# A residual sum and a value scaling moved ahead of one part of a triangular inverse in VectorE's program, in steps 2, 6 and 10

## The reference

```python
x = x + _L0_attn_ref(_layernorm(x), Wq, Wk, Wv, Wb, conv_q, conv_k, conv_v, norm_w, Wo)
x = x + _L0_ffn_ref(_layernorm(x), gate_w, expert_up_w, expert_down_w, shared_up_w, shared_down_w)

# attention: 8 heads of 64
q, k, v = (silu(conv4(x @ W)) for W in (Wq, Wk, Wv)); q, k = l2norm(q), l2norm(k)
beta = sigmoid(x @ Wb)
for each token:                                   # delta rule, S is 64 x 64 for each head
    u = beta * (v - k S); S = S + k^T u; o = q S
o = o * rsqrt(mean(o * o) + 1e-5) * norm_w;  return o @ Wo

# experts: softmax gate, 2 of 4 groups, 4 of 16 experts for a token, and a shared expert
out = sum_e cw[:, e] * (swiglu(x @ up[e].T) @ down[e].T) + swiglu(x @ shared_up.T) @ shared_down.T
```

## Time and profile before

| | us |
|---|---|
| median of three runs | 1312.88 (1310.01 to 1314.16) |
| the profiled execution | 1310.06 |
| its span, first to last instruction | 1308.3 |
| TensorE busy (matmuls) | 1263.4 |
| VectorE busy | 866.1 |
| ScalarE, GpSimd busy | 372.0, 337.8 |
| mean granted TensorE clock, share of full | 0.989 |

### The profile page before, as it was taken

One profiled execution on the slowest core, in us unless ns is written; L12 is line 12 of the kernel. 1 busy time (PEld: TensorE's weight loads), 2 busy tenths in 40 slices (PEclk: granted clock), 3 DMA queues, 4 the chain that ended last, 5 costly groups with the idle time before them and its releaser, 6 DMA issues.

```text
span 1308.3 us, 27847 instructions
## 1 busy us (share of the span) xinstructions
PE 1263.4 (97%) x8725; PEld 786.9 (60%) x8726; DVE 866.1 (66%) x2411; ACT 372.0 (28%) x818; POOL 337.8 (26%) x398
## 2 busy tenths in 40 slices
PE   7979999999999999999999999999999999999997
PEld 6857778777876565444444555555555555555553
DVE  4897698769769328363111777777777777777774
ACT  4745555655553232120000111111111111111111
POOL 1302224313242222125651112122222222121212
PEclk9989999999997999999999999999999999999999
DMA  5534943843653794585457366666665656564420
GB/s 163 91 51 97 140 112 91 170 111 78 131 122 115 169 209 105 123 265 206 177 215 248 83 132 137 131 140 137 136 140 130 137 131 135 127 139 72 75 49 9
DMA packets 208517, 171.09 MB, mean 131 GB/s; under 512 B 71473, under 2 KB 160561, under 8 KB 208433
## 3 DMA queue, kind: packets, MB, share of 16 engines
q1 hardware_dynamic: 135056, 114.16, 34.2%
q0 software_dynamic: 16496, 34.23, 13.3%
q10 hardware_dynamic: 56880, 21.54, 7.9%
HBM read 91.06 MB, written 82.73 MB: 133 GB/s over the span
## 4 chain that ended last, share of the span: by engine, by line
PE 55%; DVE 2%; issue 0%; DMA 0%; POOL 0%; ACT 0%; DVEq 0%; POOLq 0%
PE pD L2311 15%; PE pG L2286 14%; PE pU L2295 14%; PE pG L2243 3%; PE pU L2243 3%; PE pD L2262 3%; PE pU L2237 1%; PE pD L2257 0%; DVE ups L2184 0%; DMA out<-y,ix 0%; DVE w L1884 0%; DVE w L1885 0%; DVE route_keep L1883 0%; POOL out L2076 0%; DVE qf L1896 0%
## 5 line engine op out<-in xcount | busy, mean ns | idle before, releaser
L2184 DVE STREAM_TRANSPOSE ups<-a 32x96 f32<-32x96 f32 (+1 forms) x1248 | 326.1, 261 | 42.4
L2076 POOL DMA_INDIRECT out<-y,ix x79 | 123.0, 1557 | 478.9 <-ACT y L2137 313.8
L2311 PE MATMUL pD<-w,ups 128*128 (+1 forms) x474 | 216.6, 593 | 0.7 <-DVE ups L2184 0.7
L2295 PE MATMUL pU<-w,xsT 128*128 x632 | 199.9, 459 | 0.0
L2286 PE MATMUL pG<-w,xsT 128*128 x632 | 199.9, 459 | 0.0
L2286 PEld LDWEIGHTS pG<-w,xsT 128*128 128x128 f32 x632 | 119.6, 189 | 88.2 <-issue 37.6
L2295 PEld LDWEIGHTS pU<-w,xsT 128*128 128x128 f32 x632 | 120.3, 190 | 66.7
L974 PE MATMUL pProj<-front_region 128*128 128x256 f32 x624 | 154.2, 390 | 2.2 <-ACT front_region L711 1.6
L2311 PEld LDWEIGHTS pD<-w,ups 128*128 128x128 f32 (+1 forms) x474 | 90.2, 191 | 93.0 <-issue 76.7
L974 PEld LDWEIGHTS pProj<-front_region 128*128 128x128 f32 x624 | 113.1, 191 | 19.9 <-ACT front_region L711 2.1
L2137 ACT ACTIVATE y<-pD,wq 128x512 f32<-128x512 f32 x79 | 54.3, 687 | 245.3 <-PE pD L2311 235.8
(11 more groups left out here) (258 smaller groups left out, 1650.6 us busy)
## 6 DMA issues: line engine op xcount, KB each, us to landing
w<-in_up_T SPq DMA_DIRECT2D x16, 1408.0 KB, 6.9
slot_rows<-zeros SPq DMA_DIRECT2D x79, 266.0 KB, 6.8
xs<-slot_rows ACTq DMA_DIRECT2D x316, 64.0 KB
w<-in_down_T SPq DMA_DIRECT2D x16, 512.0 KB, 8.8
front_region<-in_L_attn_hidden_states SPq DMA_DIRECT2D x16, 256.0 KB, 3.7
x2r<-in_L_attn_hidden_states SPq DMA_DIRECT2D x16, 256.0 KB, 4.4
partial_sums<-x2r SPq DMA_DIRECT2D x16, 256.0 KB, 3.0
x_normed<-x2n SPq DMA_DIRECT2D x16, 256.0 KB, 2.1
```

The costliest lines, as they stand in the source:

```text
L2076: pool.indirect_dma_start(out=flat, out_offset=bass.IndirectOffsetOnAxis(ap=ix[1 - par][:, 0:1], axis=0), in_=y[1 - par][:, :], in_offset= ...
L2184: dve.transpose(aT[par][B * to:B * to + B, 0:n, rows], a[rows, 0:len(IC) * P].rearrange("p (c n) -> p c n", c=len(IC))[:, 0:n, B * to:B * ...
L2295: mm = pe.matmul(pU[0][:, 0:I], xsT[par][:, k, :], w[:, bass.ds(slot, 1), 2 * I * k + I:2 * I * (k + 1)], start=(k == 0), stop=(k == DC - 1))
L2311: mm = pe.matmul((pYlast if end(q) else pYq)[:, :], aT[1 - par][0:m, c, :], down[0:m, :, UPW + D * c:UPW + D * (c + 1)], start=(c == 0), s ...
```

## The change

VectorE's program alone is changed, and there only in order. In steps 2 and 6, `make_x2(u-1)` and `make_v(2*old)` stand in slot 4, behind the convolution of that slot and ahead of part 3 of the inverse; before, they stood in slot 5 (values first, then the residual sum), behind part 3. In step 10, `make_x2(9)` stood within part 3, behind the two multiplications; now it stands ahead of the part and of the wait that opens it.

```diff
                 if part == 3:
+                    if b == NT // 4 - 1:
+                        make_x2(NT - 7)
                     linked()
                     eight_t(0)
                     eight_t(1)
-                    if b == NT // 4 - 1:
-                        make_x2(NT - 7)
                     linked()
...
-                        if s == (4 if old == 1 else 5) and 0 < old < PAIRS - 1 and old not in LATE:
+                        if s == (4 if old == 1 else 5) and 0 < old < PAIRS - 1 and old not in LATE and u not in (2, 6):
                             make_v(2 * old)
...
-                    if s == 5 and tile_ok(u - 1) and u - 1 != NT - 7:
+                    if s == (4 if u in (2, 6) else 5) and tile_ok(u - 1) and u - 1 != NT - 7:
                         make_x2(u - 1)
+                    if s == 4 and u in (2, 6):
+                        make_v(2 * old)
```

## The result

The changed kernel has a median of 1316.58 us over 12 runs (1312.45 to 1319.83); the kernel before, 1312.64 us over 12 runs (1309.56 to 1314.31). The ratio is 1.0027 with a 95% interval of 1.0017 to 1.0038, so the change costs 3.9 us, where 1.45 us were forecast, and the interval excludes no change. A second series gave 1316.42 against 1311.96 us, 1.0028 (1.0014 to 1.0042). The profiled execution took 1315.06 us, its span 1313.3 us, 5.0 us more than that of before.

The account below looks back on a forecast made before the run. TensorE, busy 97% of the span, was taken as the bound, so only its waits for VectorE could pay. Steps 2, 6 and 10 summed as +1.45 + 0 + 0 on 1312.88, making 1314.3 us; range 1309.5 to 1317.8.

Parts of the forecast that it names:

- rival A: Slower: TensorE's single 2.68 us wait in step 7 brings the clock to 1.2 GHz, costing 3.4 us; 1317.7 us; chance 0.15.
- a low stretch near 305 us: Sign of being wrong: TensorE's granted clock shows a low stretch there, in step 7, that was not there before.
- same: Whole kernel: the measured time cannot be told from no change, within 0.3% or 3.9 us; chance 0.83.
- Step 2: VectorE waits for the output projection before the residual sum, and all that follows is late; cost +1.45 us.
- Rival D: No effect: VectorE's wait in step 2 is shorter or absorbed, steps 6 and 10 give back all; 1312.9 us; chance 0.11.
- Step 6: The merge's 2.01 us wait moves to the key transpose, which waits 2.68 us instead of 0.67; gain 0.
- Rival B: Faster: waits cut at the merge in steps 6 and 10 are partly kept, at most 3.22 us; 1311.1 us; chance 0.14.
- Step 10: The merge's wait falls from 1.97 to 0.76 us, but the wait for the scaled inverse grows by at least 1.21; gain 0.
- Rival C: Faster: less idle time keeps the clock up in step 10, gaining at most some 1.6 us; 1312.7 us; chance 0.10.

Follow-up runs that it names:

- e8_all: Kernel before with step 6's change, step 10's residual sum ahead of part 2's reduction, and part 4 of inverses behind the awaited values; 1309.08 against 1311.96 us.

## Why the prediction was right and wrong

The time of 1316.58 us lies in the range and the kernel is slower, as forecast. The size is off: +3.9 us where the sum said +1.45. That the range holds it is partly luck: its upper end is rival A, a fall of the clock at a chance of 0.15, while 0.85 us of the loss came from a clash that stands nowhere in the prediction. One of its own signs of being wrong, a low stretch near 305 us, came. The chance of 0.83 for "same" took 0.3%, 3.9 us, as the least that can be told from no change; the loss is of just that size, and with 12 runs its interval does exclude no change.

- *Step 2, +1.45.* Right: VectorE waits 1.35 us, and all behind it is 1.36 us late, in six profiles of six (1.35 to 1.36 us). No gap up to step 6 takes it up. Rival D is out.
- *Step 6, 0.* The exchange of waits was right to 0.1 us: 2.79 us in the place of 2.01 and 0.67, the values no earlier. Rival B is out, in step 10 too.
- *Step 10, 0.* Wrong, by 0.85 us. The step that failed is "does the same work in either order": the instructions are the same, but a residual sum 1.3 us earlier releases the merge and with it GpSimd's multiplication, which then runs beside VectorE's two-input multiplications. GpSimd's gets 0.46 us longer and the second of VectorE's 0.85. TensorE's wait behind it is 4.08 us: 0.46 was there, 1.33 is the earlier merge, 0.86 the later inverse, and 1.43 comes from TensorE doing what lies between at full clock, in 3.99 us in place of 5.42. I had followed what waits for the moved sum on TensorE and not one link further, to GpSimd. The Trainium skill (SBUF — State Buffer, Who interferes with whom) states it: a VectorE instruction with two inputs in SBUF contends with a GpSimd instruction that reads SBUF, a reduction does not. The trace agrees: 2.11 us beside it, 1.29 us without, and the reduction of 1.19 us untouched. The rows nearly fit turns taken whole: counted back from GpSimd's end at 404.16, its 1.05 us would begin at 403.1, about when the first multiplication ends (403.2), and the second ends 0.5 us after GpSimd's.
- *The clock, rival A.* It stood outside the sum, with a chance of 0.15, and it came. Its place was right; its price of 3.4 us was above the 1.5 to 2.9 us measured in step 7. The Trainium skill (TensorE: Matmul & The Clock Gate, HAM oscillation) tells of the clock falling in longer waits than these, waits for DMA, so it did not by itself speak for a fall at 2.68 us; the traces here show one behind 1.8 us. Two things were missing. The same holds in step 3, where I let TensorE's wait grow from 0.41 to 1.86 us and priced only the wait: in three of four profiles 1.6 us come on top. And the old order of step 7 was taken for safe from one profile; in four of five further ones it falls too, at 1.1 to 2.4 us, so what step 6 of the change adds is only the difference. By the table's means that is 2.05 - 1.17 = 0.9 us (with the first profile of before at 0 among six), and 0.75 x 1.6 = 1.2 us in step 3. This 2.1 us, which the sum put at nothing, is the largest term missing from it.
- *The sum as measured.* 1.36 + 0.85 - 0.2 (the wait in step 11 that it takes up) + 1.2 + 0.9 = 4.1 us, against 3.9 and 4.5 us in the two series. With both waits filled 1.36 + 0.85 - 0.2 = 2.0 us should be left, less the 1.2 us of falls that before has itself: 0.8 us; measured 0.4.
- *Rival C.* The clock falls in step 10 or 11 in every profile. In the kernel after it only falls later, at about 408 us for 401. Out.

What stays open: the means of the falls rest on three to six profiles, so the shares of steps 3 and 7 in the 2.1 us are not sharp. The agreement of 4.1 us with the measured times may be better than it deserves, since it leaves out the fall near 531 us: 1.66 us in two of the four profiles with the whole change's order on VectorE, in none of the other nine. Whether the change favours it isn't shown. That both waits filled together give back 4.0 us is measured; that all of it comes from steps 3 and 7 is not.

## What to carry to other kernels

When an operation is moved ahead on an engine's queue, look for what its input is waiting for at the new place, and for the next thing the waiting engine needs from the same queue: a wait that is cut in front of a second wait for the same late engine is worth nothing. Follow the released work through all engines until it stops moving, and look at which operations it now runs beside. A wait of TensorE can cost more than its length: here, in a part of the executions, the matmuls behind it ran at half the clock for 1.1 to 2.9 us more. One profile does not tell, so count the falls over several, or fill the wait once to price it.

## What the runs showed of the hardware

- The granted clock fell to 0.50 behind waits of TensorE of 1.76 us, and not always: with the same order it came in three of four profiles. Near 531 us it fell in two profiles where the last wait was 1.23 us. In step 7 one and the same order lost 0 to 2.4 us by it. Matmuls of zeros in the waits kept it up and gave back 4.0 us, with VectorE's values no sooner.
- A GpSimd multiplication of 128x512 float32, 1.05 us in the kernel before, took 1.51 us beside a pair of VectorE multiplications of 128x512, and 2.11 us for the pair in place of 1.29. The first of the pair kept its 0.66 us and the second took 1.54, as if each stood until the other engine's instruction had ended. In `e8_all` the same GpSimd multiplication took 2.66 us beside two of VectorE's, of 1.21 and 0.94 us, which took no longer than elsewhere.
- Float32 matmuls of zeros of 128 columns took 0.24 us each at full clock (3.62 us for 15), where the expectation had 0.15 us (2.3 us for 15).
